# State space stage: one token tile of four is summed by VectorE, three are weighed by ScalarE and added by GpSimd, and ScalarE scales one tile of u by B

## The chip, the core and the metric

The kernel runs on one core of a Trainium2 chip. A core has five engines that run their own instruction lists side by side and wait for each other by semaphores: TensorE (PE in the profile, its weight loads PEld), VectorE (DVE), ScalarE (ACT), GpSimd (POOL) and SyncE (SP), which here only issues DMAs. SBUF is the on-chip memory of 128 partitions, PSUM the accumulator memory that TensorE writes; GpSimd works here on SBUF alone. The metric is the device time of one execution, in microseconds (us), as the median of several runs.

## What is computed

Four layers act on x of shape (4, 1024, 256), each with layer norm ahead and a residual: a state space layer, a mixture of experts, a causal linear attention block with its feed-forward, and two layers of windowed attention with gated feed-forward. All is float32. The change lies in the first layer alone:

```
xz = jnp.einsum('bld,ed->ble', x, W_in)
u, z = jnp.split(xz, 2, axis=-1)                 # hidden = 512 each
uc = _silu(conv(u, conv_w) + conv_b)             # 3 taps along the tokens
x_dbl = jnp.einsum('blh,eh->ble', uc, W_xproj)   # 64 + 16 + 16 columns: dtp, B, C
dt = softplus(jnp.einsum('blr,hr->blh', dtp, W_dt) + b_dt)
A = -jnp.exp(A_log)                              # 16 states
def step(h, inp):
    u_t, dt_t, B_t, C_t = inp
    dA = jnp.exp(dt_t[:, None, :] * A[None, :, None])
    h = dA * h + B_t[:, :, None] * u_t[:, None, :]
    y_t = jnp.einsum('bn,bnh->bh', C_t, h)
    return (h, y_t)
y = (scan of step over the tokens) + D * uc
out = jnp.einsum('blh,dh->bld', y * _silu(z), W_out)
```

## The kernel before

`state_space_stage` works through 8 blocks of 512 tokens (N = 8, BLK = 512), two for each sequence, and for each block through the 16 states (NS). That is one loop of steps i = 16 k + n over block k and state n; every engine has its own copy of the loop (from FIRST = -20 to END), and what a block needs apart from the states is hung into the steps around it by fixed offsets r = i - 16 k. The hidden dimension of 512 lies as CT = 4 groups of 128 channels c on the partitions during the scan, and the 512 tokens as TB = 4 tiles of 128 tokens t on the partitions for everything that is weighted by B and C, since B and C then are one scalar for each partition.

One step i goes as follows.

- GpSimd scales u by B for each token tile: `ub[:, i % 2, t, :] = uT * B` (L322, `scale_u`, two steps ahead), four instructions of 128 x 512.
- TensorE turns ub into channels on partitions, four 128 x 128 transposes for each channel group, into the PSUM bank `pu[c]` (L830, `inject(i, c)`), as soon as the scan of step i - 1 has read that bank.
- ScalarE makes the decay dA = exp(dt * A) in `da`, two instructions of 128 x 1024 (L450, `step_decay`, one step ahead).
- VectorE scans each channel group along the tokens: `state = da * state + pu[c]` (L620, `scan`), four instructions of 128 x 512. In the second block of a sequence the scan starts from `carry`, which ScalarE copies after each step of the first (L455).
- TensorE turns the state back, token tile by token tile, `transpose_state(i, t)` (L842): tiles 0 and 2 go to the bank `pt[0]`, 1 and 3 to `pt[1]`.
- The output sum `acc[t] += C * state` is made in two ways. For tiles 0 and 2 VectorE does it in one instruction from `pt[0]` (L630, `add_even`). For tiles 1 and 3 ScalarE weighs `pt[1]` by C into `weighted` in SBUF (L462, `weigh`), and GpSimd adds (L336, `add_odd`).

The sum begins as D * uc (L328, `begin_sum`, GpSimd, four instructions at n = 15 of the block ahead and n = 0). In a block's steps lie, besides, the work for its neighbours: the last block's sums turned and gated (VectorE, n = 2 to 4), the next block's input product (n = 4, 5), its convolution (VectorE, L563, n = 5, 6), the product for z (n = 6, 7), the product with W_out (TensorE, n = 8, 9), Silu of uc and z on ScalarE (n = 8), the product for dt, B and C (n = 10 to 13), softplus (ScalarE, exp at n = 13, Ln at L491 at n = 14), the turned copies of u (L380, `turn_u`, n = 13 to 15), and at n = 15 the add on VectorE that completes dt (L591). ScalarE also makes the normalised input of the block after at n = 15 (L472).

All orders are written out by hand. On TensorE step i holds: state tiles 0 and 1 of step i - 1; channel groups 0 and 1 of step i + 1; state tiles 2 and 3 of step i - 1; channel groups 2 and 3 of step i + 1, with a part of the other products ahead of each channel group. At n = 15 the groups 0 and 1 come after the state tiles. Each bank may be written again only when its reader is done, so `transpose_state` for tile 2 waits for VectorE's sum of tile 0 and for tile 3 for ScalarE's weighing of tile 1.

## Time and profile before

| | |
|---|---|
| median of 3 runs | 3997.45 us (3995.81 to 3997.52) |
| the profiled execution's own time | 3997.76 us |
| its span, first to last instruction | 3995.9 us |
| mean granted TensorE clock | 0.961 |
| busy over the span: PE, DVE, ACT, POOL | 91%, 63%, 40%, 35% |
| first scan of the state space stage | 66.3 us after the span's start |
| last sum of the stage on VectorE | 1024.2 us |

In that stage the busy shares are others than over the whole span: in the page's slices VectorE stands at 8 and 9 tenths, GpSimd at 7 and 8, ScalarE at 6, TensorE at 7 and 8.

How to read the rows further below. A row of the timeline has the start in us, the duration in us, the engine, the line of the kernel, the operation, output <- inputs, the shape, and xN for N instructions in a row; a bracket tells how long the engine was idle before it, and what it waited for. A row of a group ends in `busy, mean ns | idle before, releasers`. A row of windows reads: window, its length, then busy time (and count) of PE, PEld, DVE, ACT and POOL, the granted clock, the DMA share and GB/s. Durations of neighbours on one engine overlap a little, so the step from one start to the next ("cadence") is shorter than the duration.

### The profile page before, as it was taken

Reading aid. Unit: us, or ns where it says so; the run is one execution under the profiler, and the core shown is the slowest. Engines: PE = TensorE matmul, PEld = TensorE weight load, DVE = VectorE, ACT = ScalarE, POOL = GpSimd, SP = SyncE. Lnnn points to the kernel's source line nnn. Section 1 sums busy time; section 2 is a strip of 40 time slices with the busy share of each in tenths; the row PEclk is TensorE's granted clock in tenths of the full one; section 3 lists DMA queues with packets and bytes.
Section 4 is the critical chain, followed back from the end, with each engine's and each line's share of the span. In section 5 each row is a group of like instructions: output and inputs, shape, how many; then the busy total and the mean of one; then the engine's idle time right before and its main releaser. Section 6 shows DMA issues by size and latency. Waiting matters only on the chain. (4 is left out here: it accounts for less than half of the span.)

```text
span 3995.9 us, 59179 instructions
## 1 busy us (share of the span) xinstructions
PE 3643.4 (91%) x21704; PEld 2593.4 (65%) x21704; DVE 2522.0 (63%) x5386; ACT 1601.5 (40%) x3052; POOL 1392.0 (35%) x1567
## 2 busy tenths in 40 slices
PE   6888878887799999999998998999979989999799
PEld 3666666666455688888886664666645556666465
DVE  4898988899566455555554444777743357777333
ACT  5666666666100122222221213666631146666211
POOL 4778777788100000000000223444411134444111
PEclk8899999999899999999998998999989999999899
DMA  1000000000200100000001112111122011111221
GB/s 39 1 11 12 1 11 11 11 6 6 87 32 32 35 12 12 12 12 12 11 11 55 64 63 64 38 34 37 38 63 64 27 59 33 38 34 34 74 64 37
DMA packets 150197, 129.32 MB, mean 32 GB/s; under 512 B 20804, under 2 KB 147544, under 8 KB 149656
## 3 DMA queue, kind: packets, MB, share of 16 engines
q1 hardware_dynamic: 149912, 125.54, 10.0%
q8 instruction: 177, 2.90, 0.3%
q14 instruction: 108, 0.88, 0.1%
HBM read 87.73 MB, written 37.77 MB: 31 GB/s over the span
## 5 line engine op out<-in xcount | busy, mean ns | idle before, releaser
L830 PEld LDWEIGHTS ssm_pu<-ident,ssm_ub 128*128 128x128 f32 x2048 | 255.8, 150 | 220.3 <-issue 86.0
L830 PE MATMUL ssm_pu<-ident,ssm_ub 128*128 128x128 f32 x2048 | 325.4, 292 | 80.4 <-POOL ssm_ub L322 47.2
L322 POOL TENSOR_SCALAR ssm_ub<-ssm_uT,ssm_bcT 128x512 f32<-128x512 f32 x512 | 356.4, 718 | 96.7 <-ACT ssm_uT L380 63.4
L336 POOL TENSOR_TENSOR ssm_acc<-ssm_acc,ssm_weighted 128x512 f32<-128x512 f32 x256 | 328.4, 1292 | 143.4 <-ACT ssm_weighted L462 143.0
L842 PE MATMUL ssm_pt<-ident,ssm_state 128*128 128x128 f32 x2048 | 288.5, 285 | 82.6 <-DVE ssm_acc L630 58.6
L2256 PE MATMUL win_pa<-win_w_wqkv,win_hT 128*128 128x512 f32 x768 | 357.9, 603 | 1.6 <-ACT win_hT L2043 1.1
L620 DVE TENSOR_TENSOR_SCAN ssm_state<-ssm_da,ssm_carry,ssm_pu 128x512 f32<-128x512 f32 x256 | 312.2, 1260 | 21.2 <-PE ssm_pu L830 16.4
L1838 PE MATMUL glu_up<-glu_hT,glu_w_w 128*128 128x512 f32 x704 | 309.4, 599 | 3.4 <-DVE glu_hT L1761 3.4
L620 DVE TENSOR_TENSOR_SCAN ssm_state<-ssm_da,ssm_pu 128x512 f32<-128x512 f32 x256 | 296.6, 1199 | 25.1 <-PE ssm_pu L830 16.9
L842 PEld LDWEIGHTS ssm_pt<-ident,ssm_state 128*128 128x128 f32 x2048 | 240.4, 147 | 107.9 <-DVE ssm_acc L630 67.8
L2017 POOL TENSOR_TENSOR win_rotated<-win_straight,win_turned 128x512 f32<-128x512 f32 x128 | 163.0, 1274 | 417.0 <-DVE win_turned L2132 417.0
L462 ACT ACTIVATE ssm_weighted<-ssm_pt,ssm_bcT 128x512 f32<-128x512 f32 x256 | 175.7, 686 | 319.6 <-PE ssm_pt L842 273.0
L2063 ACT ACTIVATE win_probs<-win_sc,win_nbias,win_rn 128x256 f32<-128x256 f32 x512 | 281.9, 560 | 28.9 <-DVE win_nbias L2160 21.9
L450 ACT ACTIVATE ssm_da<-ssm_dt,ssm_decay 128x1024 f32<-128x1024 f32 x256 | 292.7, 1147 | 1.4 <-DVE ssm_dt L591 1.4
L2155 DVE CUSTOM_DVE_ANT_0 win_sc<-win_sc,win_c_masks 128x256 f32<-128x256 f32 x512 | 205.7, 444 | 118.2 <-PE win_sc L2273 118.2
L1273 POOL TENSOR_TENSOR lin_rstd<-lin_mv,lin_eps 128x1 f32<-128x1 f32 x32 | 6.1, 190 | 718.2 <-DVE lin_mv L142 718.2
L1473 PE MATMUL lin_pa<-lin_hT,lin_wqk 128*128 128x128 f32 x2048 | 245.7, 278 | 3.7 <-DVE lin_hT L1362 0.8
L1838 PEld LDWEIGHTS glu_up<-glu_hT,glu_w_w 128*128 128x128 f32 x704 | 135.3, 193 | 168.3 <-issue 162.4
L1473 PEld LDWEIGHTS lin_pa<-lin_hT,lin_wqk 128*128 128x128 f32 x2048 | 233.5, 192 | 13.7 <-DVE lin_qkT L1372 8.9
L1774 DVE SCALAR_TENSOR_TENSOR glu_act<-glu_up,glu_w_b,glu_gel 128x512 f32<-128x512 f32 x96 | 71.9, 749 | 252.8 <-ACT glu_gel L1731 236.6
L1117 PE MATMUL moe_ex<-moe_w_experts,moe_hT 128*128 128x512 f32 x512 | 226.0, 594 | 0.0
L2256 PEld LDWEIGHTS win_pa<-win_w_wqkv,win_hT 128*128 128x128 f32 x768 | 138.6, 194 | 131.6 <-issue 129.7
(241 smaller groups left out, 7295.3 us busy)
## 6 DMA issues: line engine op xcount, KB each, us to landing
win_raw<-in_tables SPq DMA_DIRECT2D x64, 128.0 KB, 2.2
a<-win_y SPq DMA_DIRECT2D x64, 128.0 KB, 1.7
glu_xs<-a SPq DMA_DIRECT2D x32, 256.0 KB, 3.3
glu_x<-a SPq DMA_DIRECT2D x16, 512.0 KB, 5.3
ssm_x<-in_L_attn_x SPq DMA_DIRECT2D x8, 512.0 KB, 3.9
x<-ssm_out SPq DMA_DIRECT2D x16, 256.0 KB, 2.1
moe_x<-x SPq DMA_DIRECT2D x8, 512.0 KB, 3.9
x<-moe_y SPq DMA_DIRECT2D x8, 512.0 KB, 2.9
```

Of the source, the lines that this page charges most:

```text
L322: nc.gpsimd.tensor_scalar(ub[:, i % 2, t, :], uT[:, k % 2, t, :], bcT[:, k % 2, t, n:n + 1], 1.0, ALU.mult, ALU.mult).then_inc(ub_ready.se ...
L336: nc.gpsimd.tensor_tensor(acc[:, k % 2, t, :], acc[:, k % 2, t, :], weighted[:, j, :], ALU.add)\
L450: nc.scalar.activation(da[:, i % 2, pairs[p], :], dt[:, k % 2, pairs[p], :], ACT.Exp, scale=decay[:, n:n + 1]).then_inc(da_ready.sem, 1)
L620: nc.vector.tensor_tensor_scan(state[:, i % 2, c, :], da[:, i % 2, c, :], pu[c][:, :], carry[:, n, c:c + 1] if k % 2 else 0.0, ALU.mult, A ...
L830: last = nc.tensor.transpose(pu[c][:, t * P:(t + 1) * P], ub[:, i % 2, t, c * P:(c + 1) * P], ident)
L842: last = nc.tensor.transpose(pt[t % 2][:, c * P:(c + 1) * P], state[:, i % 2, c, t * P:(t + 1) * P], ident)
L1117: last = nc.tensor.matmul(ex[pair][:, :], hT[:, turn.side, k, t * P:(t + 1) * P], experts[:, k, pair * 2 * D:(pair + 1) * 2 * D], start=(k ...
L1473: last = nc.tensor.matmul(pa[g % 2][:, r * P:(r + 1) * P], wqk[:, g // 2, k, cols], hT[:, k, :], start=(k == 0), stop=(k == KD - 1))
L1838: last = nc.tensor.matmul(bank[:, :], w1[:, k, at:at + P], hT[:, k, :], start=(k == 0), stop=(k == KD - 1))
L2063: nc.scalar.activation(probs[:, head, :], sc[j][:, r, :], ACT.Exp, bias=nbias[:, g, j, r:r + 1], scale=rn[:, turn.side, 0, head:head + 1], ...
L2155: return nc.vector.tensor_tensor_reduce(sc[j][:, r, :], sc[j][:, r, :], mask, 1.0, -3e38, ALU.add, ALU.max, highest[:, g, j, r:r + 1])
L2256: last = nc.tensor.matmul(bank[:, :], hT[:, k, :], wqkv[:, k, g * INNER:(g + 1) * INNER], start=(k == 0), stop=(k == KD - 1))
```

## The change

VectorE sums tile 0 alone (`add_first`), and does so between its first and its second scan. Tiles 1, 2 and 3 are weighed by ScalarE (`weigh(i, t)`, tile 2 from `pt[0]`) into three buffers and added by GpSimd (`add(i, t)`). GpSimd scales tiles 0 to 2 of u by B, ScalarE scales tile 3 (`scale_last`), signalled by a semaphore of its own. The scaling on ScalarE stands at the end of a step for the step after next, at the turn of a block for the next step ahead of its decays and for the one after behind them. On TensorE the order stays, the waits ahead of the transposes of the state change. At a block's start GpSimd waits for three tiles of turned u, where it waited for four.

```
-        weighted = s.sb("weighted", [P, 2, HID])
+        weighted = s.sb("weighted", [P, TB - 1, HID])
...
             def scale_u(i):
                 k, n = divmod(i, NS)
                 if n == 0:
-                    pool.wait_ge(uT_ready.sem, uT_ready.at(k))
+                    pool.wait_ge(uT_ready.sem, uT_ready.at(k, TB - 1))
                     pool.wait_ge(bcT_ready.sem, bcT_ready.at(k))
                 pool.wait_ge(bu_made.sem, bu_made.at(i - 2))
-                for t in range(TB):
+                for t in range(TB - 1):
...
-            def add_odd(i, j):
-                k, t = i // NS, 2 * j + 1
+            def add(i, t):
+                k = i // NS
                 if i % NS == 0:
                     pool.wait_ge(begun.sem, begun.at(k))
-                pool.wait_ge(weighed.sem, weighed.at(i, j + 1))
-                pool.wait_ge(sums_odd.sem, sums_odd.at(i - 1, j + 1))
-                nc.gpsimd.tensor_tensor(acc[:, k % 2, t, :], acc[:, k % 2, t, :], weighted[:, j, :], ALU.add)\
-                  .then_inc(sums_odd.sem, 1)
+                pool.wait_ge(weighed.sem, weighed.at(i, t))
+                pool.wait_ge(sums_rest.sem, sums_rest.at(i - 1, t))
+                nc.gpsimd.tensor_tensor(acc[:, k % 2, t, :], acc[:, k % 2, t, :], weighted[:, t - 1, :], ALU.add)\
+                  .then_inc(sums_rest.sem, 1)
...
                 if 0 <= i - 1 < N * NS:
-                    add_odd(i - 1, 0)
-                    add_odd(i - 1, 1)
+                    for t in range(1, TB):
+                        add(i - 1, t)
...
-            def weigh(i, j):
-                k, t = i // NS, 2 * j + 1
-                act.wait_ge(state_turned.sem, state_turned.at(i, 2 * j + 2))
-                act.wait_ge(sums_odd.sem, sums_odd.at(i - 1, j + 1))
-                nc.scalar.activation(weighted[:, j, :], pt[1][:, :], ACT.Copy,
+            def weigh(i, t):
+                k = i // NS
+                act.wait_ge(state_turned.sem, state_turned.at(i, t + 1))
+                act.wait_ge(sums_rest.sem, sums_rest.at(i - 1, t))
+                nc.scalar.activation(weighted[:, t - 1, :], pt[t % 2][:, :], ACT.Copy,
                                      scale=bcT[:, k % 2, t, NS + i % NS:NS + i % NS + 1]).then_inc(weighed.sem, 1)
+
+            def scale_last(i):
+                k, n = divmod(i, NS)
+                if n == 0:
+                    act.wait_ge(uT_ready.sem, uT_ready.at(k))
+                    act.wait_ge(bcT_ready.sem, bcT_ready.at(k))
+                act.wait_ge(bu_made.sem, bu_made.at(i - 2))
+                nc.scalar.activation(ub[:, i % 2, TB - 1, :], uT[:, k % 2, TB - 1, :], ACT.Copy,
+                                     scale=bcT[:, k % 2, TB - 1, n:n + 1]).then_inc(ub_last.sem, 1)
...
                 if 0 <= i - 1 < N * NS:
-                    weigh(i - 1, 0)
+                    weigh(i - 1, 1)
                 second_product(i - 1)
                 if (i + 1) % NS and 0 <= i + 1 < N * NS:
                     step_decay(i + 1, 1)
                 if 0 <= i - 1 < N * NS:
-                    weigh(i - 1, 1)
+                    weigh(i - 1, 2)
+                    weigh(i - 1, 3)
                 first_product(i)
                 if (i + 1) % NS == 0 and 0 <= i + 1 < N * NS:
+                    scale_last(i + 1)
                     step_decay(i + 1, 0)
                     step_decay(i + 1, 1)
+                if (i + 2) % NS and 0 <= i + 2 < N * NS:
+                    scale_last(i + 2)
                 rest_of_step(i)
...
             for i in range(FIRST, END):
                 scanning, behind = 0 <= i < N * NS, 0 <= i - 1 < N * NS
                 if scanning:
                     scan(i, 0)
+                if behind:
+                    add_first(i - 1)
+                if scanning:
                     scan(i, 1)
                 after_second_scan(i)
-                if behind:
-                    add_even(i - 1, 0)
                 if scanning:
                     scan(i, 2)
                     scan(i, 3)
-                if behind:
-                    add_even(i - 1, 1)
                 rest_of_step(i)
...
             def inject(i, c):
                 if c == 0:
                     pe.wait_ge(ub_ready.sem, ub_ready.at(i))
+                    pe.wait_ge(ub_last.sem, ub_last.at(i))
...
             def transpose_state(i, t):
                 if t == 0:
                     pe.wait_ge(state_ready.sem, state_ready.at(i))
-                j = t // 2 + 1
-                if t % 2:
-                    pe.wait_ge(weighed.sem, weighed.at(i, j - 1) if j == 2 else weighed.at(i - 1))
+                if t == 0:
+                    pe.wait_ge(weighed.sem, weighed.at(i - 1, 2))
+                elif t == 1:
+                    pe.wait_ge(weighed.sem, weighed.at(i - 1, 3))
+                elif t == 2:
+                    pe.wait_ge(sums_first.sem, sums_first.at(i))
                 else:
-                    pe.wait_ge(sums_even.sem, sums_even.at(i, j - 1) if j == 2 else sums_even.at(i - 1))
+                    pe.wait_ge(weighed.sem, weighed.at(i, 1))
```

At the turn of the first block, step n = 15 on VectorE before; the scans are listed as scalar_tensor_tensor with output ssm_state:

```order
L620 SCALAR_TENSOR_TENSOR ssm_state<-ssm_da,ssm_pu 128x512 [waits ssm_state_turned,ssm_bu_made,ssm_carried,ssm_da_ready]
L620 SCALAR_TENSOR_TENSOR ssm_state<-ssm_da,ssm_pu 128x512 [waits ssm_bu_made]
L591 TENSOR_TENSOR ssm_dt<-ssm_dt,ssm_work 128x2048 [waits ssm_relu_ready,ssm_soft_steps]
L630 SCALAR_TENSOR_TENSOR ssm_acc<-ssm_pt,ssm_bcT,ssm_acc 128x512 [waits ssm_state_turned,ssm_sums_even]
L620 SCALAR_TENSOR_TENSOR ssm_state<-ssm_da,ssm_pu 128x512 [waits ssm_bu_made,ssm_da_ready]
L620 SCALAR_TENSOR_TENSOR ssm_state<-ssm_da,ssm_pu 128x512 [waits ssm_bu_made]
L630 SCALAR_TENSOR_TENSOR ssm_acc<-ssm_pt,ssm_bcT,ssm_acc 128x512 [waits ssm_state_turned,ssm_sums_even]
```

The same stretch of VectorE's list in the changed kernel:

```order
L634 SCALAR_TENSOR_TENSOR ssm_state<-ssm_da,ssm_pu 128x512 [waits ssm_state_turned,ssm_bu_made,ssm_carried,ssm_da_ready]
L644 SCALAR_TENSOR_TENSOR ssm_acc<-ssm_pt,ssm_bcT,ssm_acc 128x512 [waits ssm_state_turned,ssm_sums_first]
L634 SCALAR_TENSOR_TENSOR ssm_state<-ssm_da,ssm_pu 128x512 [waits ssm_bu_made]
L605 TENSOR_TENSOR ssm_dt<-ssm_dt,ssm_work 128x2048 [waits ssm_relu_ready,ssm_soft_steps]
L634 SCALAR_TENSOR_TENSOR ssm_state<-ssm_da,ssm_pu 128x512 [waits ssm_bu_made,ssm_da_ready]
L634 SCALAR_TENSOR_TENSOR ssm_state<-ssm_da,ssm_pu 128x512 [waits ssm_bu_made]
```

The sum of tile 0 (output ssm_acc) has moved from behind the add that completes dt (output ssm_dt) to ahead of it, and the second sum of the step, behind the last scan, is gone.

On ScalarE, the same turn before, from the logarithm of step 14 (output ssm_work) to the normalised input (ssm_h):

```order
L491 ACTIVATE ssm_work<-ssm_work 128x2048 [waits ssm_soft_steps]
L455 ACTIVATE ssm_carry<-ssm_state 128x4 [waits ssm_state_ready]
L462 ACTIVATE ssm_weighted<-ssm_pt,ssm_bcT 128x512 [waits ssm_sums_odd,ssm_state_turned]
L380 ACTIVATE ssm_uT<-ssm_pf 128x512 [waits ssm_uT_made]
L462 ACTIVATE ssm_weighted<-ssm_pt,ssm_bcT 128x512 [waits ssm_sums_odd,ssm_state_turned]
L380 ACTIVATE ssm_uT<-ssm_pf 128x512 [waits ssm_uT_made]
L450 ACTIVATE ssm_da<-ssm_dt,ssm_decay 128x1024 [waits ssm_state_ready,ssm_dt_ready]
L450 ACTIVATE ssm_da<-ssm_dt,ssm_decay 128x1024 [waits ssm_state_ready]
L469 ACTIVATE ssm_h_after<-ssm_x_after,ssm_shift,ssm_rstd 1x256 [waits ssm_res_ready,ssm_shift_ready]
```

And in the changed kernel:

```order
L501 ACTIVATE ssm_work<-ssm_work 128x2048 [waits ssm_soft_steps]
L456 ACTIVATE ssm_carry<-ssm_state 128x4 [waits ssm_state_ready]
L463 ACTIVATE ssm_weighted<-ssm_pt,ssm_bcT 128x512 [waits ssm_sums_rest,ssm_state_turned]
L381 ACTIVATE ssm_uT<-ssm_pf 128x512 [waits ssm_uT_made]
L463 ACTIVATE ssm_weighted<-ssm_pt,ssm_bcT 128x512 [waits ssm_sums_rest,ssm_state_turned] x2
L381 ACTIVATE ssm_uT<-ssm_pf 128x512 [waits ssm_uT_made]
L472 ACTIVATE ssm_ub<-ssm_uT,ssm_bcT 128x512 [waits ssm_bu_made,ssm_bcT_ready,ssm_uT_ready]
L451 ACTIVATE ssm_da<-ssm_dt,ssm_decay 128x1024 [waits ssm_state_ready,ssm_dt_ready]
L451 ACTIVATE ssm_da<-ssm_dt,ssm_decay 128x1024 [waits ssm_state_ready]
L472 ACTIVATE ssm_ub<-ssm_uT,ssm_bcT 128x512 [waits ssm_bu_made]
L479 ACTIVATE ssm_h_after<-ssm_x_after,ssm_shift,ssm_rstd 1x256 [waits ssm_res_ready,ssm_shift_ready]
```

Between the logarithm and the first decay of the new block stand three weighings (ssm_weighted) for two, and the scaling of the last tile of u (ssm_ub); a second scaling stands behind the decays.

## Rows read from the trace of the kernel before

**Rows 1.** Busy time by window: five stretches of a block, next turn.

```profile
538.36:550.98 12.62, 4.87 (x28) 4.11 (x27) 8.29 (x8) 7.69 (x12) 5.95 (x11) 0.70 0.01 2
550.98:585.76 34.78, 28.94 (x200) 24.54 (x199) 31.55 (x36) 19.58 (x29) 34.09 (x39) 0.91 0.00 0
585.76:604.88 19.12, 16.20 (x82) 10.33 (x81) 18.98 (x21) 12.43 (x20) 12.63 (x13) 0.91 0.01 1
604.88:641.28 36.40, 33.17 (x213) 25.91 (x211) 30.93 (x33) 24.31 (x31) 27.06 (x30) 1.00 0.10 30
641.28:660.76 19.48, 17.14 (x123) 13.36 (x122) 19.34 (x30) 18.80 (x29) 13.82 (x15) 1.00 0.00 1
660.76:673.03 12.27, 4.64 (x28) 3.90 (x27) 8.03 (x8) 7.79 (x13) 6.06 (x11) 0.72 0.00 0
```

**Rows 2.** Groups of instructions in the state space stage.

```profile
L322 POOL TENSOR_SCALAR ssm_ub<-ssm_uT,ssm_bcT 128x512 f32<-128x512 f32 x507 | 351.9, 716 | 77.8 <-ACT ssm_uT L380 44.6 <-PE ssm_pu L830 31.8
L336 POOL TENSOR_TENSOR ssm_acc<-ssm_acc,ssm_weighted 128x512 f32<-128x512 f32 x256 | 328.4, 1292 | 143.4 <-ACT ssm_weighted L462 143.0
...
L462 ACT ACTIVATE ssm_weighted<-ssm_pt,ssm_bcT 128x512 f32<-128x512 f32 x256 | 175.7, 686 | 319.6 <-PE ssm_pt L842 273.0 <-POOL ssm_acc L336 45.6
...
L380 ACT ACTIVATE ssm_uT<-ssm_pf 128x512 f32<-128x512 f32 x28 | 16.7, 597 | 0.0
```

**Rows 3.** Timeline, two half steps in the last block.

```profile
1005.71 2.44 DVE L620 TENSOR_TENSOR_SCAN ssm_state<-ssm_da,ssm_carry,ssm_pu 128x512 f32<-128x512 f32 x2
...
1008.21 0.66 PE L830 MATMUL ssm_pu<-ident,ssm_ub 128*128 128x128 f32 x4 [0.52 <-DVE ssm_state L620]
1008.71 2.44 DVE L620 TENSOR_TENSOR_SCAN ssm_state<-ssm_da,ssm_carry,ssm_pu 128x512 f32<-128x512 f32 x2
...
1008.94 1.06 PE L842 MATMUL ssm_pt<-ident,ssm_state 128*128 128x128 f32 x8
```

**Rows 4.** Timeline, the turn from block 3 into block 4.

```profile
537.69 1.92 ACT L491 ACTIVATE ssm_work<-ssm_work 128x2048 f32<-128x2048 f32 x1
...
538.36 2.44 DVE L620 TENSOR_TENSOR_SCAN ssm_state<-ssm_da,ssm_carry,ssm_pu 128x512 f32<-128x512 f32 x2
...
540.27 0.59 ACT L380 ACTIVATE ssm_uT<-ssm_pf 128x512 f32<-128x512 f32 x1
540.72 2.26 DVE L591 TENSOR_TENSOR ssm_dt<-ssm_dt,ssm_work 128x2048 f32<-128x2048 f32 x1
...
543.70 1.97 PE L842 MATMUL ssm_pt<-ident,ssm_state 128*128 128x128 f32 x8 [3.61 <-DVE ssm_acc L630]
545.71 0.69 ACT L462 ACTIVATE ssm_weighted<-ssm_pt,ssm_bcT 128x512 f32<-128x512 f32 x1 [4.85 <-PE ssm_pt L842]
...
546.29 0.59 ACT L380 ACTIVATE ssm_uT<-ssm_pf 128x512 f32<-128x512 f32 x1
...
546.98 2.69 POOL L322 TENSOR_SCALAR ssm_ub<-ssm_uT,ssm_bcT 128x512 f32<-128x512 f32 x4 [6.59 <-ACT ssm_uT L380]
...
549.64 2.50 POOL L336 TENSOR_TENSOR ssm_acc<-ssm_acc,ssm_weighted 128x512 f32<-128x512 f32 x2
...
550.98 2.33 DVE L620 TENSOR_TENSOR_SCAN ssm_state<-ssm_da,ssm_pu 128x512 f32<-128x512 f32 x2 [4.34 <-PE ssm_pu L830]
```

**Rows 5.** Timeline, TensorE, the same place one step apart.

```profile
609.13 1.04 PE L842 MATMUL ssm_pt<-ident,ssm_state 128*128 128x128 f32 x8
...
616.07 1.04 PE L842 MATMUL ssm_pt<-ident,ssm_state 128*128 128x128 f32 x8
```

**Rows 6.** Timeline, TensorE behind the two Silu calls of ScalarE.

```profile
626.04 0.65 PE L842 MATMUL ssm_pt<-ident,ssm_state 128*128 128x128 f32 x4 [2.42 <-ACT ssm_weighted L462]
```

**Rows 7.** Timeline, convolutions on VectorE, the second beside an add on GpSimd.

```profile
593.28 1.76 DVE L563 SCALAR_TENSOR_TENSOR ssm_uc<-ssm_u,ssm_conv_w,ssm_uc 128x512 f32<-128x512 f32 x2
...
597.21 2.52 DVE L563 SCALAR_TENSOR_TENSOR ssm_uc<-ssm_u,ssm_conv_w,ssm_uc 128x512 f32<-128x512 f32 x2
...
597.49 1.69 POOL L336 TENSOR_TENSOR ssm_acc<-ssm_acc,ssm_weighted 128x512 f32<-128x512 f32 x1
```

31 lines of the change are left out of this document (16 added, 15 removed).

## Prediction, made before the change was run

> **What bounds the kernel now.** I read the groups of instructions first, then the waits, then windows over one block, then the timeline at the places where the windows show loss. Only the state space stage changes. Its 128 steps start at 66.3 us and its last sum starts at 1024.2 us. Steps are numbered n = 0 to 15 within a block. One block runs from scan to scan in 122.05 us (550.98 to 673.03) [rows 1]; no engine owns it, the bound moves:
>
> - Plain steps belong to VectorE. Two scans take 2.44 us and the next pair starts 3.00 us after the first, so one summing instruction takes 0.56 us of cadence, and a step is 2 x 3.00 = 6.0 us in a block with carried states [rows 3]. In a fresh block the pair takes 2.33 [rows 4], a step 2 x 2.89 = 5.8.
> - Steps n = 0 to 4 (34.78 us) belong to GpSimd, busy 34.09 [rows 1].
> - Steps 5 and 6 (19.12) are VectorE's with its convolutions, busy 18.98 [rows 1].
> - Steps 7 to 11 (36.40) are TensorE's: the same eight transposes return after 6.94 us, whatever the others do [rows 5]. In one step TensorE waits 2.42 us for ScalarE, behind the two Silu calls [rows 6].
> - Steps 12 to 14 (19.48) are shared, VectorE 19.34 and ScalarE 18.80 busy [rows 1].
> - Step 15, the turn, is a chain in which all wait (12.62, then 12.27) [rows 1]. The rows of [rows 4] give it: VectorE adds dt (540.72, 2.26 us) ahead of its sum of tile 0; TensorE may turn tiles 2 and 3 only after that sum (idle 3.61); ScalarE weighs tile 3 at 545.71 (idle 4.85) and only then copies the last tiles of u; GpSimd waits 6.59 us for them, scales four tiles, and the scans start at 550.98.
>
> **The change, part by part.**
>
> *VectorE* loses one sum per step, 128 in all, 0.56 us each. If all of it counted, 128 x 0.56 = 72 us. Against that stands a new wait. The one sum left follows the first scan directly, and it needs tile 0 turned. TensorE first puts in the fourth group for the scan (starts 0.06 us after the scan ends at 1008.15, 0.73 us until the state transposes start at 1008.94), then turns tile 0 (some 0.6 for four of the eight): ready at about 1009.54, while the sum could start at 1009.33 [rows 3]. So some 0.25 us is lost per step: VectorE 5.45 us in a fresh step, 5.7 in a carried one. At the lower clock eight transposes take 1.97 instead of 1.06 [rows 3, 4], which would make it some 0.7.
>
> *GpSimd* loses one scaling of four, gains one add on two. Four scalings are 2.69 us, two adds 2.50 [rows 4]: 0.67 and 1.25 each. Its step goes from 5.19 to 3 x 0.67 + 3 x 1.25 = 5.76, +0.57. A plain step is therefore GpSimd's afterwards, at 5.8: no gain on 5.8, 0.2 on 6.0.
>
> *ScalarE* gains one weighing (0.69 alone, 0.58 in cadence: the copy behind the one at 545.71 begins at 546.29) [rows 4] and one scaling of u. No row shows that scaling. Its neighbours are the copy of a tile from PSUM (0.60) and the weighing with its scale operand (0.69) [rows 2], so 0.5 to 0.7 of cadence; I take 0.55, as for the copy. Together 1.15 us a step, 18.4 us a block.
>
> *TensorE* does the same work. Tile 2 now waits for VectorE's single sum, which comes early, tile 3 for weighing tile 1, tiles 0 and 1 of the next step for the weighings of tiles 2 and 3.
>
> Now by stretch of the block, before against after:
>
> 1. Turn, 12.4 on average. After, the sum of tile 0 is ahead of the dt add, so TensorE's tiles 2 and 3 and ScalarE's weighings don't wait for it, and GpSimd needs only the three tiles that come out of the copy at 540.27 [rows 4], not the last one. What is late next is ScalarE: with 18.80 busy in 19.48 us [rows 1] (about 16 of cadence) it gets 3 x 1.15 less 0.55 (no scaling falls on n = 14) = 2.9 more in steps 12 to 14, fills them, and ends its logarithm at about scan start + 5.0 instead of + 1.25 (537.69 + 1.92 - 538.36). Then: weigh and copy of u to + 6.1; the dt add, which needs the logarithm, + 5.1 to + 7.3; scans 2 and 3 to + 9.7; meanwhile GpSimd scales to + 8.1 and ScalarE to + 8.5 and decays to + 9.5. The next scan starts at + 9.7: **-2.7**. With a prompt ScalarE it is VectorE's list alone, 4.9 + 0.56 + 2.2 + 0.3 = 7.9 (-4.5); with a later one 0.
> 2. Steps 0 to 4, 34.8. From the first scaling to the end of the sixth GpSimd now works 6 x 2.69 + 4 x 2.50 + 2 x 2.50 (the four begins of the sums, at the price of adds) = 31.1, after 6 x 2.0 + 4 x 3.75 + 5.0 = 32.0. But it starts at + 6.1 of the turn instead of + 8.6 (546.98 - 538.36), and VectorE no longer stands behind tile 2. Followed queue by queue: **-1.5**. Bounds: VectorE's own load is 5 x 5.45 + 4 gates at the price of a sum, 0.6 = 29.7 (-5); GpSimd's 0.57 x 5 unhidden is +2.9.
> 3. Steps 5 and 6: VectorE's, the new wait is covered by the convolutions behind the scans: -0.57 each, less some collision, **-0.9** (-1.1 to 0).
> 4. Steps 7 to 11: TensorE's 6.94 stays; the wait behind the Silu calls gets 0.55 to 1.15 longer, VectorE's first scan runs ahead in it: **+0.1** (-0.5 to +1.5).
> 5. Steps 12 to 14: VectorE 0.3 less each, ScalarE's 2.9 mostly pushed into the turn, where it is counted: **-0.9** (-1.6 to +2.4).
>
> Sum -5.9 a turn block, times 7 = -41. The last block has 11 plain carried steps more, 0.2 each: -2. The first block's start and the last sums nearly cancel.
>
> One collision has to be added. In [rows 7] a pair of convolutions takes 2.52 instead of 1.76 while an add of GpSimd takes 1.69 instead of 1.25: two inputs from SBUF on VectorE and GpSimd get in each other's way. Today the dt add (2.26, two SBUF inputs) runs while GpSimd is idle (6.59 before its scaling) [rows 4]; after, GpSimd is in its first scaling from + 6.1 with the dt add until + 7.3. I charge 0.7 us per turn: 7 x 0.7 = 5. The Trainium skill, page "SBUF — State Buffer", section "SBUF: two separate sides", says that VectorE with two SBUF inputs and a GpSimd instruction that reads SBUF take the shared ports in turn, the later one fully blocked. By that rule the price would be up to one whole dt add a turn; the rows agree that both lengthen.
>
> Sum: -41 - 2 + 5 = -38. The profiled execution took 3997.76 us (its span 3995.9, 1.9 around it), 0.3 above the median: 3997.8 - 38 = 3959.8, as a median 3959.5.
>
> **The rivals.**
>
> - *VectorE's own list decides everywhere* (chance 0.12). ScalarE stays prompt since its durations overlap, GpSimd catches up in the convolution steps. Then -4.5 - 5 - 1.1 - 0.5 - 1.6 = -12.7 a block, 7 x 12.7 = 89: 3909. For it: ScalarE idles 273 us for TensorE before weighing [rows 2]. Against: 34.09 of 34.78 busy on GpSimd, whose list grows [rows 1].
> - *Port collisions and a late u eat the turn* (0.14). A full dt add, 2.26, is lost to GpSimd each turn and 1.5 more to longer adds beside it and the convolutions: -5.9 + 3.8 = -2.1 a block, with the last block -17: 3980. For it: [rows 7]. Half of this case's span lies within 0.2%.
> - *ScalarE becomes the bound* (0.12), the slow side. TensorE now needs a weighing for three tiles of four, and by the same following of queues only some 1.2 us lie between the weighing of tile 2 and the need for it, where VectorE used to read tile 2 itself. If ScalarE's list between two such weighings exceeds about 5.8 us, every us of it shows. In steps 7 to 14 it is busy 43.11 of 55.88 [rows 1], and all 8 steps might pay 1.15: +9.2 a block, 8 blocks +74; less turns 7 x 2.7 and steps 0 to 6 7 x 2.4, 38 remain: 4036.
> - *The change doesn't do what it says*: excluded by the order of instructions, which has one sum after the first scan and ScalarE's scaling where it was put.
>
> **How the numbers follow.** My forecast case (3930 to 3988) has 0.62. Faster by over 0.2% (8 us, about what a measurement of this kernel can tell from no change): 0.62 + 0.12 + half of 0.14 = 0.81. Within: 0.07. Slower: 0.12. The range reaches from 3928, part of the way to the first rival, to 3990, past the second; the sum of all upper bounds (0 + 2.9 + 0 + 1.5 + 2.4 a block) belongs to the slow rival and stays out.
>
> **What would show it.** The turn windows shrink from 12.4 to about 9.7 us, GpSimd's idle before its scaling (6.59) mostly goes, and so does ScalarE's 4.85. VectorE's sum shows idle of about 0.25 us for TensorE in plain steps. Plain steps of the last block stand at 5.8. Steps 7 to 11 stay at 36.4. GpSimd's adds have waits of less than the 143 us of [rows 2] per added call, ScalarE's idle for TensorE falls well below 273. I am wrong if the turn stays at 12, if steps 12 to 14 take over 21 us, or if TensorE's waits for the weighings, now short, grow to a us per step.

## The result and the profile after

The changed kernel takes 4007.53 us (median of 8 runs, 3998.98 to 4019.51), the kernel before 3995.62 (8 runs, 3992.77 to 3997.52). The ratio is 1.0032, 95% interval 1.002 to 1.0044: slower by 0.3%, where 3959.5 and "faster" were forecast. The result lies outside the range (3928 to 3990), on the other side of zero. The spread over its runs is 20 us; the kernel before has 5.

The profiled execution of the changed kernel took 4009.6 us (span 4007.8). In it the scans run from 64.6 to 1036.5 us, before from 66.3 to 1018.9: the state space stage became 19.3 us longer. The work outside it, which the change does not touch, took 7.4 us less than in the profile of before (3035.9 against 3043.3); over the other kernels of this study it lies between 3033.5 and 3044.9, so I read nothing into it. The middle block again, from scan to scan, cut at the same steps as [rows 1] (columns as there):

```profile
546.80:555.83 9.03, 4.53 (x36) 3.53 (x34) 7.88 (x8) 9.00 (x13) 8.13 (x11) 0.99 0.01 4
555.83:589.88 34.05, 28.09 (x198) 24.39 (x198) 28.57 (x30) 26.98 (x43) 34.05 (x37) 0.90 0.00 1
589.88:615.30 25.42, 19.28 (x98) 12.86 (x96) 23.46 (x19) 16.60 (x27) 17.04 (x18) 0.87 0.00 1
615.30:653.27 37.97, 32.82 (x197) 25.25 (x196) 27.34 (x28) 28.92 (x40) 27.89 (x28) 0.96 0.10 29
653.27:672.87 19.60, 16.77 (x117) 12.50 (x116) 17.70 (x26) 19.60 (x32) 14.89 (x15) 1.00 0.00 1
672.87:682.12 9.25, 4.74 (x38) 3.74 (x36) 7.61 (x7) 9.22 (x14) 8.35 (x11) 0.99 0.00 1
```

Against [rows 1]: the turn 12.62 and 12.27 -> 9.03 and 9.25, steps 0 to 4 34.78 -> 34.05, steps 5 and 6 19.12 -> **25.42**, steps 7 to 11 36.40 -> 37.97, steps 12 to 14 19.48 -> 19.60. VectorE's busy time in steps 5 and 6 rose from 18.98 to 23.46 although it has two sums fewer there. One block may be a bad sample, so all further comparisons use the mean of blocks 1 to 6 (worked out from the starts of the first scan of each step, us; the last column is the sum of the 64 convolution instructions of the run):

```
                  0-4    5-6    7-11   12-14  15     block  convolutions
before            35.22  19.39  36.39  19.28  12.62  122.9  62.8
after             34.25  23.95  37.88  19.88   9.35  125.3  91.6
forecast for it   33.7   18.5   36.5   18.4    9.9
```

(The forecast row is the row of before with the prediction's five terms added, the 0.7 for the collision left out.) One number carries the result: +4.6 us in steps 5 and 6, in the first block (+4.3) as in the others, 7 x 4.56 = 32 us. The convolutions took 29 us more.

**The turn** came out as forecast. Timeline, the same turn as [rows 4]:

```profile
548.59 0.75 DVE L644 SCALAR_TENSOR_TENSOR ssm_acc<-ssm_pt,ssm_bcT,ssm_acc 128x512 f32<-128x512 f32 x1 [0.52 <-PE ssm_pt L859]
...
550.60 2.31 DVE L605 TENSOR_TENSOR ssm_dt<-ssm_dt,ssm_work 128x2048 f32<-128x2048 f32 x1
550.93 0.71 ACT L381 ACTIVATE ssm_uT<-ssm_pf 128x512 f32<-128x512 f32 x1
...
551.20 0.66 PE L859 MATMUL ssm_pt<-ident,ssm_state 128*128 128x128 f32 x4 [1.15 <-ACT ssm_weighted L463]
...
551.82 1.15 POOL L309 TENSOR_TENSOR ssm_shift<-ssm_shift,ssm_rstd 128x5 f32<-128x5 f32 x1
...
552.96 2.02 POOL L323 TENSOR_SCALAR ssm_ub<-ssm_uT,ssm_bcT 128x512 f32<-128x512 f32 x3
...
555.83 1.22 DVE L634 TENSOR_TENSOR_SCAN ssm_state<-ssm_da,ssm_pu 128x512 f32<-128x512 f32 x1 [0.55 <-PE ssm_pu L844]
```

The sum of tile 0 is through before the add that completes dt (L605). TensorE, which waited 3.61 us for that sum in [rows 4], now waits 1.15 and for ScalarE. GpSimd starts to scale at 552.96, 2.9 us ahead of the scans, in [rows 4] 4.0 ahead; the scans start after an idle of 0.55 us where it was 4.34.

**The plain steps** of the last block, the place of [rows 3]:

```profile
1014.37 2.42 DVE L634 TENSOR_TENSOR_SCAN ssm_state<-ssm_da,ssm_carry,ssm_pu 128x512 f32<-128x512 f32 x2
...
1016.88 0.75 DVE L644 SCALAR_TENSOR_TENSOR ssm_acc<-ssm_pt,ssm_bcT,ssm_acc 128x512 f32<-128x512 f32 x1
...
1017.55 4.78 DVE L634 TENSOR_TENSOR_SCAN ssm_state<-ssm_da,ssm_carry,ssm_pu 128x512 f32<-128x512 f32 x4
1017.72 2.02 POOL L323 TENSOR_SCALAR ssm_ub<-ssm_uT,ssm_bcT 128x512 f32<-128x512 f32 x3
...
1022.41 0.75 DVE L644 SCALAR_TENSOR_TENSOR ssm_acc<-ssm_pt,ssm_bcT,ssm_acc 128x512 f32<-128x512 f32 x1
...
1023.42 2.03 POOL L323 TENSOR_SCALAR ssm_ub<-ssm_uT,ssm_bcT 128x512 f32<-128x512 f32 x3
```

From sum to sum 5.53 us, where [rows 3] gave 6.00 and the forecast was 5.8. GpSimd's cycle is 1023.42 - 1017.72 = 5.70 here: it falls 0.17 us behind per step, which the few steps shown don't yet feel.

**The convolutions** are where the time went. Timeline of the changed kernel in steps 5 and 6, GpSimd's rows and those around them:

```profile
588.45 2.03 POOL L323 TENSOR_SCALAR ssm_ub<-ssm_uT,ssm_bcT 128x512 f32<-128x512 f32 x3
...
590.44 3.75 POOL L337 TENSOR_TENSOR ssm_acc<-ssm_acc,ssm_weighted 128x512 f32<-128x512 f32 x3
...
593.67 7.55 DVE L577 SCALAR_TENSOR_TENSOR ssm_uc<-ssm_u,ssm_conv_w,ssm_uc 128x512 f32<-128x512 f32 x2
...
594.16 2.05 POOL L323 TENSOR_SCALAR ssm_ub<-ssm_uT,ssm_bcT 128x512 f32<-128x512 f32 x3
...
596.15 3.73 POOL L337 TENSOR_TENSOR ssm_acc<-ssm_acc,ssm_weighted 128x512 f32<-128x512 f32 x3
...
602.40 1.12 PE L844 MATMUL ssm_pu<-ident,ssm_ub 128*128 128x128 f32 x4 [5.87 <-DVE ssm_state L634]
...
606.18 2.02 POOL L323 TENSOR_SCALAR ssm_ub<-ssm_uT,ssm_bcT 128x512 f32<-128x512 f32 x3 [6.30 <-PE ssm_pu L844]
```

Two convolutions (L577) together take 7.55 us; the pair of [rows 7] took 1.76. GpSimd goes from 588.45 to 599.88 (596.15 + 3.73) without a gap, three scalings, three adds, three scalings, three adds (and was busy without one in all of steps 0 to 4, 34.05 of 34.05), and the pair ends at 601.22, that is 1.34 after GpSimd's last add. Everything then stands: TensorE waits 5.87 us for a scan that VectorE couldn't start, and comes back at the lower clock (four matmuls in 1.12 where 0.60 to 0.66 is usual; granted clock of the window 0.87). GpSimd waits 6.30 us for TensorE. The same line over the stage, first before, then after (min, median, max in ns):

```profile
L563 DVE SCALAR_TENSOR_TENSOR ssm_uc<-ssm_u,ssm_conv_w,ssm_uc x56: 721/853/4276, 96.0 to 849.8; 128x512 f32<-128x512 f32 x56
```

```profile
L577 DVE SCALAR_TENSOR_TENSOR ssm_uc<-ssm_u,ssm_conv_w,ssm_uc x56: 718/915/6760, 95.3 to 866.8; 128x512 f32<-128x512 f32 x56
```

The shortest is the same, 0.72 us. The longest went from 4.28 to 6.76 us. Of the 56 convolutions 8 took more than 2 us, 39.7 us together; before, one did. Six of these 8 end 0.55 us after the last instruction of GpSimd's unbroken run; the other two (2.21 and 2.52 us) got in inside the run.

GpSimd of the kernel before at this place:

```profile
590.35 1.26 POOL L336 TENSOR_TENSOR ssm_acc<-ssm_acc,ssm_weighted 128x512 f32<-128x512 f32 x1
592.43 1.27 POOL L336 TENSOR_TENSOR ssm_acc<-ssm_acc,ssm_weighted 128x512 f32<-128x512 f32 x1 [0.82 <-ACT ssm_weighted L462]
594.33 3.20 POOL L322 TENSOR_SCALAR ssm_ub<-ssm_uT,ssm_bcT 128x512 f32<-128x512 f32 x4 [0.62 <-PE ssm_pu L830]
...
602.36 1.27 POOL L336 TENSOR_TENSOR ssm_acc<-ssm_acc,ssm_weighted 128x512 f32<-128x512 f32 x1 [3.18 <-ACT ssm_weighted L462]
605.92 0.70 POOL L322 TENSOR_SCALAR ssm_ub<-ssm_uT,ssm_bcT 128x512 f32<-128x512 f32 x1 [2.30 <-PE ssm_pu L830]
```

It has gaps in each step, 0.82 and 3.18 us for ScalarE's weighing, 0.62 and 2.30 for TensorE. After the change it has none in the twelve instructions above. The list of the waits in the stage points the same way (us in total, times, longest):

```profile
POOL ssm_acc L337 <- ACT ssm_weighted L463: 121.7, 72, 3.7
```

121.7 us over 384 adds, where [rows 2] has 143.0 over 256: 0.32 an add instead of 0.56.

### The profile page after: what moved, and what is told of

Its sections match the earlier page's. It is cut to its first block and busy times, and to the rows that moved or that the text cites. A ratio compares the mean times of both kernels' runs of the same rounds, so it can differ in the third digit from the quotient of the medians.

```text
span 4007.8 us, 59443 instructions
## 1 busy us (share of the span) xinstructions
PE 3639.8 (91%) x21704; PEld 2595.4 (65%) x21704; DVE 2473.9 (62%) x5258; ACT 1749.6 (44%) x3308; POOL 1464.1 (37%) x1567
## 5 line engine op out<-in xcount | busy, mean ns | idle before, releaser
L337 POOL TENSOR_TENSOR ssm_acc<-ssm_acc,ssm_weighted 128x512 f32<-128x512 f32 x384 | 481.7, 1277 | 122.6 <-ACT ssm_weighted L463 121.7
L463 ACT ACTIVATE ssm_weighted<-ssm_pt,ssm_bcT 128x512 f32<-128x512 f32 x384 | 253.0, 695 | 172.5 <-PE ssm_pt L859 138.3
L859 PE MATMUL ssm_pt<-ident,ssm_state 128*128 128x128 f32 x2048 | 286.4, 284 | 37.4 <-ACT ssm_weighted L463 33.7
L323 POOL TENSOR_SCALAR ssm_ub<-ssm_uT,ssm_bcT 128x512 f32<-128x512 f32 x384 | 268.5, 717 | 63.4 <-PE ssm_pu L844 43.9
L859 PEld LDWEIGHTS ssm_pt<-ident,ssm_state 128*128 128x128 f32 x2048 | 245.1, 147 | 46.3 <-ACT ssm_weighted L463 37.9
L1748 ACT ACTIVATE glu_gel<-glu_up,glu_w_b 128x512 f32<-128x512 f32 x96 | 65.9, 686 | 387.0 <-PE glu_up L1855 387.0
```

What stands on the lines that cost most here:

```text
L323: nc.gpsimd.tensor_scalar(ub[:, i % 2, t, :], uT[:, k % 2, t, :], bcT[:, k % 2, t, n:n + 1], 1.0, ALU.mult, ALU.mult).then_inc(ub_ready.se ...
L337: nc.gpsimd.tensor_tensor(acc[:, k % 2, t, :], acc[:, k % 2, t, :], weighted[:, t - 1, :], ALU.add)\
L463: nc.scalar.activation(weighted[:, t - 1, :], pt[t % 2][:, :], ACT.Copy, scale=bcT[:, k % 2, t, NS + i % NS:NS + i % NS + 1]).then_inc(wei ...
L859: last = nc.tensor.transpose(pt[t % 2][:, c * P:(c + 1) * P], state[:, i % 2, c, t * P:(t + 1) * P], ident)
```

## Experiments

Three theories were open. **A, the lock**: a VectorE instruction with two SBUF inputs and GpSimd's instructions exclude one another, and with ScalarE feeding it ahead of VectorE, GpSimd leaves no gap. (These are two claims: that there is a lock, and why it costs more after the change. The next runs test the first.) **B, ScalarE**: the added scaling delays the weighings that TensorE waits for. **C, GpSimd's list**: its 0.57 us more a step costs directly, and the long convolution is only a symptom. All ratios are against the kernel before on the same chip; the mean block of every kernel stands in one table at the end of this section.

### The convolution's second input out of SBUF

```diff
-                    nc.vector.scalar_tensor_tensor(uc[:, c, :], u[:, c, tap:tap + BLK], conv_w[:, c, tap:tap + 1],
-                                                   uc[:, c, :], ALU.mult, ALU.add).then_inc(conv_steps.sem, 1)
+                    nc.vector.scalar_tensor_tensor(uc[:, c, :], u[:, c, tap:tap + BLK], conv_w[:, c, tap:tap + 1],
+                                                   uc[:, c, :] if bank is None else bank[:, :], ALU.mult, ALU.add)\
+                      .then_inc(conv_steps.sem, 1)
...
-                        convolve(k, 2 * (r + 11))
+                        if k:
+                            dve.wait_ge(bu_made.sem, bu_made.at(i, 3))
+                        convolve(k, 2 * (r + 11), pu[2] if k else None)
...
-                        convolve(k, 2 * (r + 11) + 1)
+                        if k:
+                            dve.wait_ge(bu_made.sem, bu_made.at(i + 1, 1))
+                        convolve(k, 2 * (r + 11) + 1, pu[0] if k else None)
```

`bank` is one of the PSUM banks of pu, for blocks 1 to 7, with a wait until it is filled. The running sum of the taps is thereby left out of the result; the count and size of the instructions stay. First on the changed kernel (a_psum):

> The changed kernel, in which the second input of the convolution on VectorE is a PSUM bank in place of the SBUF tile it adds to (for blocks 1 to 7; so the addition of the centre tap is left out and the values differ). Number, length and waits of the instructions stay. Theory P (a VectorE instruction with two SBUF inputs stands still while GpSimd works without a gap): the 91.6 us that the convolutions take in the changed kernel fall to about 45, steps 5 and 6 from 24.0 to about 18.5 us a block, and the kernel takes 3965 to 3975 us. Rival L (what is lost in steps 5 and 6 is ScalarE's later copies of u, or another wait): no change, 4003 to 4010.

Measured 3961.45 us (3960.86 to 3966.85, 4 runs), ratio 0.9913 (0.9899 to 0.9928): 1.19% or 47 us below the changed kernel. Timeline and the line's spread:

```profile
570.30 1.50 DVE L577 SCALAR_TENSOR_TENSOR ssm_uc<-ssm_u,ssm_conv_w,ssm_pu 128x512 f32<-128x512 f32 x2
570.43 2.02 POOL L323 TENSOR_SCALAR ssm_ub<-ssm_uT,ssm_bcT 128x512 f32<-128x512 f32 x3
...
572.43 3.74 POOL L337 TENSOR_TENSOR ssm_acc<-ssm_acc,ssm_weighted 128x512 f32<-128x512 f32 x3
...
573.96 1.50 DVE L577 SCALAR_TENSOR_TENSOR ssm_uc<-ssm_u,ssm_conv_w,ssm_pu 128x512 f32<-128x512 f32 x2
```

```profile
L577 DVE SCALAR_TENSOR_TENSOR ssm_uc<-ssm_u,ssm_conv_w,ssm_pu x56: 719/736/749, 97.0 to 819.4; 128x512 f32<-128x512 f32 x56
```

GpSimd works through the convolutions just as closely (570.43 to 576.17), and each of the 56 takes 0.72 to 0.75 us. Steps 5 and 6 take 17.00 instead of 23.95. GpSimd's list is the same as in the changed kernel, so for these steps theory C falls; the lock stands. The same edit on the kernel before (b_psum):

> The kernel before with the same edit (centre tap left out of the addition, PSUM bank as second input). Theory P: its convolutions take 62.8 us, of which about 15 are waits beside GpSimd; 1 to 2 us a block, so 3981 to 3990 us. Rival L: 3994 to 3997.

Measured 3978.18 us (3976.71 to 3979.04, 4 runs), ratio 0.9951 (0.9935 to 0.9968). The kernel before pays for the lock too: 19 us, 15 of them seen in the convolutions (56.8 -> 41.4 us). The change raised that price by the rest, 1.19% - 0.49% = 0.7% or 28 us, give or take some 10 by the intervals of the ratios.

### A gap held open for the convolutions

In steps 5 and 6 of the changed kernel GpSimd waits, ahead of its adds, until the first two convolutions of the step are done (a_hold).

```diff
+                for k in range(N):
+                    if k and i - k * NS in (-11, -10):
+                        pool.wait_ge(conv_steps.sem, conv_steps.at(k, 4 * (i - k * NS + 11) + 2))
                 if 0 <= i - 1 < N * NS:
```

> The changed kernel, in which GpSimd waits in steps 5 and 6 ahead of its adds until the first two convolution instructions of that step are done; nothing is left out. Theory P (a convolution can't start while GpSimd runs without a gap, and waits for the end of the whole run): the 6 to 7 us convolution goes, steps 5 and 6 fall from 24.0 to 18 or 19 us a block, the kernel takes about 3972 us. Rival: GpSimd's list is so full that what the wait costs it comes back in the following steps: 3990 us or more.

Measured 3995.77 us (3992.31 to 3997.46, 10 runs), ratio 0.9995 (0.9985 to 1.0004).

```profile
585.93 3.52 DVE L580 SCALAR_TENSOR_TENSOR ssm_uc<-ssm_u,ssm_conv_w,ssm_uc 128x512 f32<-128x512 f32 x2
...
586.08 2.05 POOL L323 TENSOR_SCALAR ssm_ub<-ssm_uT,ssm_bcT 128x512 f32<-128x512 f32 x3
...
589.54 4.18 POOL L337 TENSOR_TENSOR ssm_acc<-ssm_acc,ssm_weighted 128x512 f32<-128x512 f32 x3 [1.41 <-DVE ssm_uc L580]
```

The first convolution still stands behind the three scalings (585.93, the pair ends at 589.45), and then GpSimd stands for 1.41 us. The convolutions total 77.6 us instead of 91.6, steps 5 and 6 take 21.43. 0.37% or 15 us came back, a third of what the PSUM input gives, and the time lies where the rival of the expectation had it (3990 or more): the run of scalings ahead of the hold is still there, and the wait costs GpSimd time. Nothing is left out of the computation here, so the gap alone gave the 15 us.

### The turn alone

The kernel before, with the sum of tile 0 ahead of the dt add, but still behind the second scan, and nothing else (b_reorder):

```diff
-                after_second_scan(i)
                 if behind:
                     add_even(i - 1, 0)
+                after_second_scan(i)
```

> The kernel before, only VectorE's first sum (tile 0) moved ahead of what follows the second scan (dt add, convolution, gates). Theory T (the 3.3 us that the turn lost came from TensorE standing behind the dt add): turns fall from 12.6 to about 9.5 us, 7 x 3 = 21, the kernel takes about 3975 us. Rival U (they came from GpSimd waiting for three tiles of u and no longer four, or from the smaller list of VectorE): turns stay near 12, the kernel within 5 us of 3995.6.

Measured 3975.64 us (3973.24 to 3977.46, 4 runs), ratio 0.9946 (0.9931 to 0.996). Timeline of the turn:

```profile
530.34 0.73 DVE L630 SCALAR_TENSOR_TENSOR ssm_acc<-ssm_pt,ssm_bcT,ssm_acc 128x512 f32<-128x512 f32 x1
530.98 2.29 DVE L591 TENSOR_TENSOR ssm_dt<-ssm_dt,ssm_work 128x2048 f32<-128x2048 f32 x1
...
531.13 1.09 PE L842 MATMUL ssm_pt<-ident,ssm_state 128*128 128x128 f32 x8 [1.41 <-DVE ssm_acc L630]
...
533.53 2.71 POOL L322 TENSOR_SCALAR ssm_ub<-ssm_uT,ssm_bcT 128x512 f32<-128x512 f32 x4 [3.51 <-ACT ssm_uT L380]
...
537.55 2.33 DVE L620 TENSOR_TENSOR_SCAN ssm_state<-ssm_da,ssm_pu 128x512 f32<-128x512 f32 x2 [1.27 <-PE ssm_pu L830]
```

TensorE waits 1.41 us instead of 3.61 and the turn takes 9.59 instead of 12.62 on average. So two lines that changed places are enough for nearly the whole gain of the turn; neither the third weighing nor the scaling is needed for it.

### Tile 3 of u to ScalarE

The kernel before takes over from the change only what concerns u (b_scale): `scale_last`, its place at the end of ScalarE's step, three scalings on GpSimd, which waits for three tiles of turned u, and TensorE's second wait.

```diff
-                    pool.wait_ge(uT_ready.sem, uT_ready.at(k))
+                    pool.wait_ge(uT_ready.sem, uT_ready.at(k, TB - 1))
...
-                for t in range(TB):
+                for t in range(TB - 1):
...
                 if (i + 1) % NS == 0 and 0 <= i + 1 < N * NS:
+                    scale_last(i + 1)
...
+                if (i + 2) % NS and 0 <= i + 2 < N * NS:
+                    scale_last(i + 2)
...
+                    pe.wait_ge(ub_last.sem, ub_last.at(i))
```

> The kernel before with tile 3 of u scaled by ScalarE in all steps and nothing else. GpSimd's list in steps 0 to 4 is what bounds them (34.1 of 34.8 us busy): they fall by 2.4 us a block, and the turn by one scaling (0.7) and the weighings ahead; steps 7 to 14 grow by 1.5. Sum -2 us a block, about 3980. If the turn needs both edits to move, it stays at 12 us.

Measured 3976.76 us (3973.89 to 3981.08, 4 runs), ratio 0.995 (0.9935 to 0.9965). Steps 0 to 4 fall from 35.22 to 32.75, the turn to 10.65, steps 7 to 11 rise by 0.9. The turn thus gains 2.0 us from this edit too, without the change of order. Together with the change of order (b_reorder_scale):

> The kernel before with that reordering, and tile 3 of u scaled by ScalarE instead of GpSimd as in the change; the sums stay two on VectorE, two on GpSimd. Theories T and P together: GpSimd's list falls to 4.5 us a step, steps 0 to 4 gain 2 us, convolutions less held: about 3960 us. Rival S (ScalarE's 0.6 us a step is what costs): steps 7 to 11 grow by 1.5 us a block as in the change and 3975 or more comes out.

Measured 3947.57 us (3942.62 to 3955.18, 4 runs), ratio 0.9877 (0.9863 to 0.9892). Singly the two give 0.54% and 0.50%, together 1.23%, no less than their sum; the 0.19% above it lies within the intervals. The convolutions of this kernel:

```profile
L576 DVE SCALAR_TENSOR_TENSOR ssm_uc<-ssm_u,ssm_conv_w,ssm_uc x56: 731/752/1448, 95.2 to 807.3; 128x512 f32<-128x512 f32 x56
```

None is longer than 1.45 us, though their second input is in SBUF. GpSimd has one instruction less per step and still waits for weighings behind VectorE's two sums.

The other way round, the changed kernel with all four scalings on GpSimd, which waits again for four tiles of turned u (a_scale_back):

```diff
-                    pool.wait_ge(uT_ready.sem, uT_ready.at(k, TB - 1))
+                    pool.wait_ge(uT_ready.sem, uT_ready.at(k))
...
-                for t in range(TB - 1):
+                for t in range(TB):
...
-                    scale_last(i + 1)
...
-                if (i + 2) % NS and 0 <= i + 2 < N * NS:
-                    scale_last(i + 2)
...
-                    pe.wait_ge(ub_last.sem, ub_last.at(i))
```

> The changed kernel with the scaling of tile 3 of u given back to GpSimd (four scalings and three adds there, 6.4 us a step; ScalarE only has the third weighing more than before). Theory P: GpSimd's runs get longer, the convolutions take over 100 us in all, steps 0 to 4 grow by 2 to 3 us a block, the kernel takes 4020 to 4050 us. Theory S (ScalarE's extra work is what costs in steps 7 to 14): these steps fall by 1 to 2 us a block; if S were the larger part, the kernel would be below 4007.

Measured 4023.07 us (4019.43 to 4025.29, 4 runs), ratio 1.0062 (1.0047 to 1.0077). Steps 0 to 4 as a window:

```profile
563.10:600.25 37.15, 30.27 (x199) 26.63 (x198) 28.69 (x30) 22.32 (x34) 37.15 (x41) 0.85 0.00 0
```

GpSimd is busy in all of it, 37.15 against 34.05 in the changed kernel. Steps 7 to 11, on the other hand, take 35.66 instead of 37.88, steps 12 to 14 19.30 instead of 19.88: there ScalarE's scaling costs 2.8 us a block. That is theory B, for a smaller share of the loss.

### ScalarE scales only where it has time

States 0 to 8 of each block are scaled as in the change, for states 9 to 15 GpSimd scales all four tiles, tile 3 first (a_mix).

```diff
+        LIGHT = 9
...
-                for t in range(TB - 1):
+                for t in range(TB - 1) if n < LIGHT else (3, 0, 1, 2):
...
             def scale_last(i):
                 k, n = divmod(i, NS)
+                if n >= LIGHT:
+                    return
...
-                    pe.wait_ge(ub_ready.sem, ub_ready.at(i))
-                    pe.wait_ge(ub_last.sem, ub_last.at(i))
+                    k, n = divmod(i, NS)
+                    mine = LIGHT * k + min(n + 1, LIGHT)
+                    pe.wait_ge(ub_ready, 4 * (i + 1) - mine)
+                    if n < LIGHT:
+                        pe.wait_ge(ub_last, mine)
```

> The changed kernel, in which ScalarE scales tile 3 of u only for the states 0 to 8; for 9 to 15 GpSimd does it. Theory S (ScalarE's scalings around its Silu, exp and Ln calls cost in steps 7 to 14): steps 7 to 11 fall from 37.9 to 35.7 us a block and 12 to 14 from 19.9 to 19.3, 8 x 2.8 = 22 us, the kernel takes about 3985 us. Rival (these steps lose by the third weighing or by TensorE's waits, not by the scaling): no change there, GpSimd's longer list costs, 4005 to 4015.

Measured 3996.1 us (3986.6 to 4006.52, 10 runs), ratio 0.9998 (0.9988 to 1.0009), 0.34% or 14 us below the changed kernel, where about 22 were expected. The profiled execution is the slowest of the ten (4006.5), so its table row shows the bad side: steps 7 to 11 fell by 1.4, 12 to 14 by 0.8, but steps 5 and 6 rose by 1.3, with the longest convolution at 7.78 us. With two causes in one kernel this run separates nothing. Therefore the same with the second input in PSUM (the running sum of the taps left out as above; a_mix_psum), beside a_psum:

> The changed kernel with both edits: the convolution's second input from a PSUM bank (the centre tap is left out of its addition for blocks 1 to 7), and ScalarE scaling tile 3 of u for the states 0 to 8 only. Without the long convolutions (a_psum, 3961.5 us) what the ScalarE scalings cost in steps 7 to 14 must show by itself. Theory S: steps 7 to 11 fall from 38.1 to about 36.5, 12 to 14 from 20.0 to 19.1, some 2.5 us a block, the kernel takes about 3941 to 3947 us. Rival (ScalarE's scalings cost nothing by themselves): 3958 to 3965.

Measured 3942.28 us (3941.4 to 3950.26, 4 runs), ratio 0.9871 (0.9855 to 0.9887): 0.42% or 17 us below a_psum (19 by the medians). Steps 7 to 11 and 12 to 14 as windows, first a_psum, then this kernel:

```profile
583.36:621.35 37.99, 33.74 (x203) 25.76 (x200) 27.36 (x28) 29.37 (x40) 28.27 (x29) 0.96 0.10 29
621.35:640.95 19.60, 16.77 (x117) 12.50 (x116) 17.71 (x25) 19.60 (x32) 14.90 (x15) 1.00 0.00 1
```

```profile
571.69:609.05 37.36, 33.73 (x202) 25.81 (x200) 27.35 (x28) 27.04 (x36) 31.78 (x34) 0.95 0.09 29
609.05:628.54 19.49, 17.00 (x115) 13.31 (x114) 17.67 (x25) 19.28 (x31) 16.78 (x18) 0.95 0.01 2
```

On average 38.08 -> 36.78 and 19.99 -> 19.29, 2.0 us a block. ScalarE's busy time in steps 7 to 11 is 2.3 lower, GpSimd's 3.5 higher, and it is faster: the bound there passes through ScalarE. On the fastest kernel so far, b_reorder_scale, the same edit (b_mix):

> The reordered kernel before with tile 3 of u scaled by ScalarE for the states 0 to 8 only. Theory S: steps 7 to 11 go from 37.0 back to 35.8 us, the gain in steps 0 to 6 stays: 3936 to 3942. Rival: GpSimd's longer list in steps 7 to 14 costs the same, 3947 or more.

Measured 3947.39 us (3942.43 to 3948.92, 4 runs), ratio 0.9877 (0.986 to 0.9893), no different from 3947.57: the 6 to 12 us that I expected are not there. That ScalarE, with one weighing less per step, has the room is my reading; no run shows it by itself.

### Does a longer list on GpSimd do it by itself

The kernel before with one spare 128 x 512 scaling per step on GpSimd, 0.67 us (b_extra):

```diff
                     add_odd(i - 1, 1)
+                    if i > 1:
+                        pool.wait_ge(spared.sem, spared.at(i - 2))
+                    nc.gpsimd.tensor_scalar(spare[:, 1, :], spare[:, 0, :], 1.0, 1.0, ALU.mult, ALU.mult).then_inc(spared.sem, 1)
```

> The kernel before with one more scaling of 128x512 on GpSimd in each step (a spare tile that nobody reads, 0.67 us), so its list is 5.9 us a step, as long as in the change, with nothing changed on VectorE, ScalarE or TensorE. Theory P: the convolutions grow from 62.8 us in all to 80 or more, steps 5 and 6 by 3 us or more a block, and steps 0 to 4 by 0.6 us a step: 4025 to 4045 us. Rival (the long convolution needs the new order on VectorE or ScalarE): convolutions stay at 63, only steps 0 to 4 grow: 4005 to 4020.

Measured 4008.0 us (4006.68 to 4011.38, 10 runs), ratio 1.0025 (1.0016 to 1.0035). GpSimd's list is now longer than in the changed kernel, 4 + 1 scalings and 2 adds or 5.85 us against 5.76, yet the convolutions total 72.3 us, not 91.6, the longest 2.38, and steps 5 and 6 rise by 1.4, not 4.6. So it isn't the length of the list alone. Here GpSimd's adds still wait for weighings that stand behind VectorE's own sums: when VectorE is held up, GpSimd soon runs out of work and lets VectorE in. In the changed kernel ScalarE weighs three tiles that wait on no sum of VectorE after the first, and GpSimd can run on for six more instructions while VectorE stands. This reading fits both kernels, but no run shows it by itself.

The single instructions of the traces also say that a closed run of GpSimd isn't enough. I count the convolutions that began beside a running GpSimd instruction with at least two more behind it, each less than 0.05 us after the last. In b_extra 37 did, and 33 of them got in at the next boundary; in b_reorder_scale all of 14, with 3.0 to 3.5 us of GpSimd's run still ahead; in the kernel before 11 of 12. In the changed kernel only 9 of 18 did. So the change made long waits frequent, and the lock is what they wait for, but what makes half of them miss the boundary is open. The change also puts the sum between the first two scans and moves tile 2's sum away from VectorE, which shifts where the convolutions fall; no run takes these apart.

### The hold on the best kernel

b_reorder_scale with the wait of a_hold (best):

> The reordered kernel before with tile 3 of u scaled by ScalarE (3947.6 us), and the same wait of GpSimd ahead of its adds in steps 5 and 6. Theory P: its convolutions take 56.0 us in all, of which 8 are waits; half goes: 3942 to 3947. Rival: the wait costs GpSimd as much as it spares VectorE: 3947 to 3955.

Measured 3951.73 us (3948.93 to 3954.92, 4 runs), ratio 0.9884 (0.987 to 0.9899). The profiled block is 0.7 us shorter (115.8), the runs are not faster: where there is no long lock, the hold has nothing to give.

### All kernels side by side

Mean of blocks 1 to 6 between starts of the first scans, from the profiled executions; "over 2" counts the convolutions longer than 2 us among the 56 in the stage:

```
                  0-4    5-6    7-11   12-14  15     block  conv.  over 2  ratio
before            35.22  19.39  36.39  19.28  12.62  122.9  62.8   1       1
b_psum            34.94  17.52  35.83  19.28  12.58  120.2  47.4   0       0.9951
b_reorder         35.40  19.23  35.76  19.28   9.59  119.3  61.5   1       0.9946
b_scale           32.75  19.53  37.31  19.53  10.65  119.8  60.9   0       0.9950
b_reorder_scale   32.80  18.77  36.96  19.53   8.42  116.5  56.0   0       0.9877
b_mix             33.03  18.75  36.63  19.28   8.33  116.0  55.9   0       0.9877
best              32.84  18.19  36.72  19.53   8.55  115.8  52.5   0       0.9884
b_extra           35.93  20.80  35.83  19.28  12.33  124.2  72.3   7       1.0025
after             34.25  23.95  37.88  19.88   9.35  125.3  91.6   8       1.0032
a_hold            34.10  21.43  37.26  20.33   9.44  122.6  77.6   7       0.9995
a_mix             33.91  25.26  36.49  19.05   9.22  123.9  98.5   8       0.9998
a_scale_back      37.07  23.37  35.66  19.30  10.60  126.0  93.2   9       1.0062
a_psum            34.06  17.00  38.08  19.99   9.48  118.6  47.2   0       0.9913
a_mix_psum        33.87  17.01  36.78  19.29   9.30  116.2  47.2   0       0.9871
```

The fastest version that computes everything is b_reorder_scale (or b_mix): 3947.5 us, 1.2% below the kernel before. It has tile 0's sum ahead of the dt add and the change's scaling on ScalarE, and leaves tile 2's sum on VectorE.

## Why the prediction was wrong

Point by point, by its own steps (mean block, forecast against measured):

1. *Turn, -2.7.* Measured -3.3. Right, and its reason, the order of the sum and the dt add, is enough by itself (b_reorder, -3.0). It isn't the only one: b_scale without that order gives -2.0.
2. *Steps 0 to 4, -1.5.* Measured -1.0, GpSimd without a gap in 34.05 us. Right. What hid in it: the scaling moved away is worth -2.5 (b_scale), and the moved sum with its third add gives 1.5 of that back (b_reorder_scale against the changed kernel).
3. *Steps 5 and 6, -0.9 (-1.1 to 0).* Measured **+4.6**. **This is the step that failed.** It read "VectorE's, the new wait is covered by the convolutions behind the scans: -0.57 each, less some collision". The collision was the term.
4. *Steps 7 to 11, +0.1 (-0.5 to +1.5).* Measured +1.5, the upper bound. The mechanism was named (the wait behind the Silu calls), its size was off; a_psum against a_mix_psum prices ScalarE's scaling at 1.3 here, a_scale_back at 2.2.
5. *Steps 12 to 14, -0.9 (-1.6 to +2.4).* Measured +0.6. ScalarE is busy 19.60 of 19.60 in the first window table. "Mostly pushed into the turn" was wrong by that 0.6, and VectorE's 0.3 less a step did not come through. The third weighing seems to cost nothing here: without the scaling these steps take 19.30, as before (a_scale_back).
6. *Last block, -2.* The plain steps gave 0.46 us each rather than 0.2, since the expected idle of 0.25 ahead of VectorE's sum isn't there (the sum starts at 1016.88, 0.09 after the scans' end), but the steps with input projections lost more; the block went from 97.0 to 97.7.

None of the three signs that were to show the forecast wrong came. The turn stands at 9.35 us, steps 12 to 14 at 19.88, and TensorE's waits for the weighings (L859) went from 21.7 to 33.7 us over 128 steps. All three watched ScalarE and the turn, none the convolutions.

**The failed step in detail.** The rows were on the table. [rows 7] shows a pair of convolutions 0.76 us longer beside an add 0.44 us longer, and the prediction drew the right rule from it: VectorE with two SBUF inputs and GpSimd get in each other's way. Two things went wrong behind that. First, the place. The 0.7 us a turn was charged at the dt add, because there GpSimd's work was to come to lie beside it. The turn after shows what that cost: the dt add stays at 2.31 us, and what stands is a small GpSimd instruction (L309, 1.15 us, where it takes 0.20 in b_reorder, ahead of the dt add and as L308) and then the first scaling, which starts at 552.96, at the dt add's end of 552.91. The turn gained in full all the same. The convolutions, where VectorE was the bound and had no slack, got "some collision". Second, the size. I took one GpSimd instruction as the most that a collision could last, and the rival with its 1.5 us a block for "adds and convolutions" did so as well. The step where it decided has single waits of up to 6 us.

The Trainium skill, page "SBUF — State Buffer", section "SBUF: two separate sides", says that the shared pair of ports is an exclusive lock, held by whoever starts first for its whole instruction, while the other is fully blocked. An estimate by that rule with this case's durations: a convolution waits for one GpSimd instruction, 1.28 us if it is an add (the mean of L337), and a pair takes up to 2 x (1.28 + 0.73) = 4.0 us. The trace agrees that one excludes the other, and goes beyond it in length: the 6.76 us convolution was passed over by six further GpSimd instructions. The measurement decides.

**The budget of the error.** Forecast -38, measured +12.8 (0.32% of 3997): 51 us. The lock's added price is 28 us (a_psum and b_psum), of which the forecast had 5, at the dt add: 23. ScalarE's scaling in steps 7 to 14 is 17 to 19 (a_mix_psum against a_psum), of which the forecast had 0.1 a block: 16 to 18. That makes 39 to 41. The rest, 10 to 12 us, is what the smaller differences of the points above, first and last block included, and the spread of the runs leave; no run splits it further. Checked from the other side: with the lock and that scaling both out of the way the change is worth 0.9951 - 0.9871 = 0.8%, 32 us, where the forecast without its collision term was 43, 11 more. All these differences carry the intervals of their ratios, some 6 to 10 us each, and in the profiles the stage grew by 19.3 us where the whole grew by 12.8.

**The rivals.** "Port collisions and a late u eat the turn" had the right mechanism with less than a third of the size, 1.5 us a block beside the dt add's 2.26, where steps 5 and 6 alone came out 5.5 above their term. "ScalarE becomes the bound" was the slow side, and its sign came true, but not its mechanism: it wanted 1.15 us in each of 8 steps, 9.2 a block, and the runs show 2.0 to 2.8 a block. The row behind it, TensorE behind the Silu calls, compare [rows 6]:

```profile
627.56 0.72 ACT L472 ACTIVATE ssm_ub<-ssm_uT,ssm_bcT 128x512 f32<-128x512 f32 x1
...
628.30 1.28 ACT L504 ACT_TABLE_LOAD   x1
...
636.49 0.66 PE L859 MATMUL ssm_pt<-ident,ssm_state 128*128 128x128 f32 x4 [3.17 <-ACT ssm_weighted L463]
...
637.35 1.22 DVE L634 TENSOR_TENSOR_SCAN ssm_state<-ssm_da,ssm_pu 128x512 f32<-128x512 f32 x1 [2.72 <-PE ssm_pt L859]
...
641.97 0.75 DVE L644 SCALAR_TENSOR_TENSOR ssm_acc<-ssm_pt,ssm_bcT,ssm_acc 128x512 f32<-128x512 f32 x1 [3.40 <-PE ssm_pt L859]
```

The scaling (L472) stands ahead of the table load and the Silu calls; TensorE waits 3.17 us instead of 2.42, the 0.75 of one scaling, and VectorE stands idle 2.72 and 3.40 us after it. "VectorE's own list decides everywhere" is out: VectorE is busy 112.56 us of the 135.32 in the first window table. What should have warned me is a remark in the prediction's own list: GpSimd's wait for the weighings shrinks. I counted it as idle time won. It was also time in which VectorE could start a convolution at once.

## What to carry to other kernels

GpSimd's idle time may be what VectorE lives on: before filling it, look for VectorE instructions with two SBUF inputs in the same stretch, and bound the collision from above by the longest unbroken run of GpSimd, not by one instruction; between the two it came out anywhere here. Where such an instruction stands on the bound, one of its inputs in PSUM removed the wait (the runs here left a sum out to get there). Keeping GpSimd's supply tied to the engine that it blocks went with short waits; that it causes them is not shown. And take a change of three parts apart before judging it: here the change of order gave 0.54%, the moved scaling 0.50%, and what is left of the change, tile 2's sum moved away and tile 0's put ahead of the second scan, took back all of it and more.

## What the hardware showed that I had not expected

- A VectorE convolution with two SBUF inputs can be passed over by six GpSimd instructions in a row (6.76 us, in a_mix up to 7.78), and the wait then ends with GpSimd's run. But not always: in other places it got in at the next boundary between two GpSimd instructions that stood as close, and then the GpSimd instruction was the longer one (the second pair of [rows 7], where the add took 1.69 instead of 1.25). In a_scale_back 7 convolutions took 3.9 to 4.0 us each: they began beside an add, were passed over by two more, and got in ahead of the next scaling, with that scaling and four more GpSimd instructions close behind. What decides this the runs don't show; it stays open.
- The same instruction with its second input in PSUM took 0.72 to 0.75 us in all 56 cases (a_psum), though 51 of them began beside a running GpSimd instruction.
- The changed kernel spreads over 20.5 us (8 runs) and a_mix over 20 (10 runs), the kernel before over 5 (8 runs), a_psum over 6 (4 runs). That the lock does this is likely, not shown: b_reorder_scale has no long convolution in its profile and spreads over 12.5 (4 runs).
- ScalarE's scaling of an SBUF tile into SBUF, with a scale per partition, took 0.728 us on average, against 0.60 for its copy of a tile from PSUM [rows 2]; the forecast had taken the copy's price. Groups of instructions of the changed kernel, its row for L472 (busy us, mean ns, idle before):

```profile
L472 ACT ACTIVATE ssm_ub<-ssm_uT,ssm_bcT 128x512 f32<-128x512 f32 x128 | 93.2, 728 | 0.3
```
